# A fused attention and quantised-MLP layer: stationary latents with streamed probabilities, and a rounding add moved to GpSimd

## What is computed

```python
xn   = (x - mean(x)) / sqrt(var(x) + 1e-5)
# attention: 8 heads of 64, keys and values from a latent of rank 64
q    = xn @ Wq.T;  latent = xn @ Wkv_down.T
k, v = latent @ Wk_up.T, latent @ Wv_up.T
attn = softmax(q @ k.T / 8) @ v @ Wo.T
# MLP of width 704 whose four operands are quantised to an fp4 grid in blocks of 16 columns
def fp4(a):                       # scale = max|block| / 6; round to 0, .5, 1, 1.5, 2, 3, 4, 6
    ...
h    = silu(fp4(xn) @ fp4(w_gate).T) * (fp4(xn) @ fp4(w_up).T)
out  = x + attn + fp4(h) @ fp4(w_down).T
```

## Time and profile before

| | |
|---|---|
| median of 3 runs | 1689.79 us (1688.26 to 1696.55) |
| the profiled execution's own time | 1696.03 us |
| its span (first to last instruction) | 1694.0 us |
| mean granted PE clock | 0.974 of full speed |
| busy: PE, DVE, ACT, POOL | 1577.0, 1340.1, 708.9, 517.8 us |

### The profile page before, as it was taken

The page is one execution under the profiler, slowest core; times in us unless marked ns, Lnnn a source line. Parts: engine busy times, 40 slices in busy tenths (PEclk is TensorE's granted clock), DMA queues, the critical chain, the costliest instruction groups (busy, mean ns, idle before and its releaser), DMA issues.

```text
span 1694.0 us, 30412 instructions
## 1 busy us (share of the span) xinstructions
PE 1577.0 (93%) x10726; PEld 1442.1 (85%) x10726; DVE 1340.1 (79%) x3368; ACT 708.9 (42%) x1382; POOL 517.8 (31%) x696
## 2 busy tenths in 40 slices
PE   0599999999999999999999999999999999999998
PEld 0488998989889898988989899898989989898897
DVE  8788787888888888888878788878888877787663
ACT  2444444444444444444443444444344444344432
POOL 7433232332232233323223323223233322332211
PEclk9799999999999999999999999999999999999999
DMA  3000000000000000000000000000000000000000
GB/s 98 7 10 4 8 20 4 19 8 11 14 8 17 7 20 7 10 14 7 17 7 20 4 14 14 8 17 7 20 5 14 14 4 20 7 11 8 1 14 13
DMA packets 22885, 22.60 MB, mean 13 GB/s; under 512 B 3280, under 2 KB 22224, under 8 KB 22736
## 3 DMA queue, kind: packets, MB, share of 16 engines
q1 hardware_dynamic: 22736, 20.65, 4.0%
HBM read 11.99 MB, written 8.39 MB: 12 GB/s over the span
## 4 chain that ended last, share of the span: by engine, by line
PE 87%; DVE 9%; issue 3%; ACT 1%; DMA 0%; POOL 0%; SPq 0%; DVEq 0%; POOLq 0%
PE m L774 35%; PE po L904 23%; PE mx L863 7%; PE st L889 7%; PE st L890 6%; PE m L876 3%; PE m L1010 2%; PE m L1016 1%; PE m L928 1%; DVE row_max L611 1%; PE m L1024 1%; DVE hid L595 1%; DVE on_lo L745 1%; DVE h_small L583 1%; DVE x_small L583 1%
## 5 line engine op out<-in xcount | busy, mean ns | idle before, releaser
L904 PEld LDWEIGHTS po<-lat_tok,probs 128*128 128x128 f32 x4096 | 523.5, 194 | 22.9
L904 PE MATMUL po<-lat_tok,probs 128*128 128x65 f32 x4096 | 519.1, 270 | 0.0
L506 ACT ACTIVATE probs<-st 128x512 f32<-128x512 f32 x512 | 291.3, 595 | 338.2 <-PE st L890 338.2
L611 DVE TENSOR_REDUCE row_max<-mx 128x1 f32<-128x512 f32 x512 | 327.7, 682 | 0.6 <-PE mx L863 0.6
L411 POOL TENSOR_TENSOR h_norm<-hid,h_small 128x352 f32<-128x352 f32 x128 | 100.8, 788 | 480.7 <-DVE h_small L588 480.7
L889 PE MATMUL st<-q_hi,lat 128*128 128x512 f32 x512 | 212.7, 415 | 0.0
L890 PE MATMUL st<-q_lo,lat 65*128 65x512 f32 x512 | 203.6, 398 | 0.0
L774 PE MATMUL m<-wgu_hi,xt_hi 128*128 128x352 f32 x512 | 191.9, 375 | 0.1
L724 DVE TENSOR_TENSOR q_lo<-m,q_hi 64x512 fp32r<-64x512 f32 x128 | 88.1, 688 | 122.4 <-ACT q_hi L546 122.4
L442 POOL TENSOR_TENSOR h_norm<-h_norm,hid 128x352 f32<-128x352 f32 x128 | 119.7, 935 | 211.6 <-DVE h_norm L597 211.6
L863 PE MATMUL mx<-lat,q_hi 128*128 128x512 f32 x512 | 176.5, 426 | 4.0 <-DVE row_max L611 3.9
(11 more groups left out here) (178 smaller groups left out, 3054.2 us busy)
## 6 DMA issues: line engine op xcount, KB each, us to landing
x_in<-in_L_attn_x_dram SPq DMA_DIRECT2D x64, 128.0 KB, 2.2
out_dram<-acc SPq DMA_DIRECT2D x32, 256.0 KB, 2.3
q_lo<-neg_max SPq DMA_DIRECT2D x128, 2.0 KB
weights_in<-in_L_ffn_w_down_dram SPq DMA_DIRECT2D x1, 704.0 KB, 6.3
weights_in<-in_L_ffn_w_gate_dram SPq DMA_DIRECT2D x1, 640.0 KB, 4.7
acc<-in_L_ffn_w_up_dram SPq DMA_DIRECT2D x1, 640.0 KB, 5.9
wq_in<-in_L_attn_Wq_dram SPq DMA_DIRECT2D x1, 512.0 KB, 5.9
x_in<-in_L_attn_Wo_dram SPq DMA_DIRECT2D x1, 512.0 KB, 7.0
```

Of the source, the lines that this page charges most:

```text
L506: act.activation(probs[:, t.c % 2, kc, :], st[kc % 2][:, :], ACT.Exp).then_inc(exp_done, 1)
L611: dve.tensor_reduce(row_max[:, u.c % 2, qc:qc + 1], mx[qc % 2][:, :], AX.X, ALU.max).then_inc(mx_taken, 1)
L904: last = pe.matmul(po[:, qc * P:qc * P + R + 1], probs[:, u.c % 2, kc, qc * P:(qc + 1) * P], lat_tok[:, s.c % 2, kc, 0:R + 1], start=(kc = ...
```

## The change

Five things, in one edit.

1. **Weighing.** `weigh` runs once for two heads, in even slots. `lat_tok` (64 columns) is stationary and `probs` streams: 512 fp32 columns for each block of 128 keys. The first head writes partitions 0 to 63 of `po`, the second 64 to 127, and the two alternate. The result has features on the partitions, as the output product wants it, and the transposes of L1016 go.
2. **Denominators.** POOL adds the four key blocks of `probs` (`add_keys`, three adds of 128x512 for a head); PE multiplies the sum by the ones column, with the sum stationary (64 columns with a stride of 8) and one moving column (`weights_sum`, 16 matmuls for a pair); DVE takes the reciprocal; SP stores it to DRAM and reads it back spread over 64 partitions (`inv_b`); DVE multiplies `po` by it in the next slot; two slots later ACT and POOL split it into `on_hi` and `on_lo`.
3. **Queries.** ACT copies the query product in one piece of 128 partitions (`qp_hi`), DVE makes `qp_lo` in one, and SP places them by six DMAs for a pair. The product itself stands earlier in the slot.
4. **Quantisation.** The rounding constant comes from ACT (a square and a copy with a bias, to bf16), and POOL adds it, where DVE did all three steps. Chunks are normalised two slots earlier.
5. **Order.** The down product is done once for both halves, in odd slots; the residual is loaded into `acc` by a DMA of its own; gate, up and the transposes of maxima and hidden chunk stand together; `wov` moves one slot later. There are 14 lead and 6 tail slots.

```diff
-        on = sb("on", [P, 2, CH, P])
+        on = sb("on", [P, T])
+        inv_b = sb("inv_b", [P, T])
+        key_sum = sb("key_sum", [P, 2, T])
...
+            def place_query(m, u):
+                h = 2 * m.c % QH + u
+                sp.wait_ge(q_hi_done, m.n(1, 1))
+                if u and m.over(2).any():
+                    sp.wait_ge(st_psum, m.n(2 * CH, -2 * CH))
+                for v in range(2):
+                    sp.dma_start(q_hi[v * R:(v + 1) * R, h, :].bitcast(F32), qp_hi[u * R:(u + 1) * R, :].bitcast(F32)).then_inc(q_hi_placed[u], 16)
+                sp.wait_ge(q_lo_done, m.n(1, 1))
+                sp.dma_start(q_lo[0:R, h, :].bitcast(F32), qp_lo[u * R:(u + 1) * R, :].bitcast(F32)).then_inc(q_lo_placed[u], 16)
...
+                m = scaled_pair(t)
+                if m is not None:
+                    sp.wait_ge(inv_done, m.n(1, 1))
+                    sp.dma_start(inv_rows[m.c % 2].rearrange("v (p j) -> (v p) j", p=R), inv_den[:, m.c % 2, :]).then_inc(inv_stored, 16)
...
+                if m is not None:
+                    sp.wait_ge(inv_stored, m.n(16, 16))
+                    for v in range(2):
+                        sp.dma_start(inv_b[v * R:(v + 1) * R, :],
+                                     inv_rows[m.c % 2, v:v + 1, :].broadcast_to([R, T])).then_inc(inv_spread, 16)
...
+            def add_keys(t, kc):
+                total, last = key_sum[:, t.c % 2, :], probs[:, t.c % 2, kc, :]
+                pool.wait_ge(exp_done, t.n(CH, kc + 1))
...
+                pool.tensor_tensor(total, first, last, ALU.add).then_inc(sum_step, 1)
...
-                    pool.wait_ge(h_round, w.n(ROUND_STEPS, ROUND_STEPS))
+                    pool.wait_ge(h_magic_done, w.n(1, 1))
...
-                    pool.tensor_tensor(h_norm[:, :], h_norm[:, :], hid[:, w.c % 2, :], ALU.subtract).then_inc(h_grid, 1)
+                    pool.tensor_tensor(h_norm[:, :], h_norm[:, :], h_magic[:, :], ALU.add).then_inc(h_round, 1)
+                    pool.wait_ge(h_round, w.n(1, 1))
+                    pool.tensor_tensor(h_norm[:, :], h_norm[:, :], h_magic[:, :], ALU.subtract).then_inc(h_grid, 1)
...
+                    act.activation(hid[:, w.c % 2, :], h_norm[:, :], ACT.Square, scale=MAGIC_SQUARE).then_inc(h_square, 1)
+                    act.wait_ge(h_square, w.n(1, 1))
+                    act.activation(h_magic[:, :], hid[:, w.c % 2, :], ACT.Copy, bias=MAGIC_LEAST).then_inc(h_magic_done, 1)
...
+            def weigh(t):
+                m = weighed_pair(t)
+                if m is not None:
...
+                    for kc in range(CH):
+                        pe.wait_ge(exp_done, m.n(2 * CH, CH + kc + 1))
+                        for v in range(2):
+                            last = pe.matmul(po[v * R:(v + 1) * R, :], lat_tok[:, s.c % 2, kc, 0:R], probs[:, v, kc, :],
+                                             start=(kc == 0), stop=(kc == CH - 1))
+                        last.then_inc(pv_done, 1)
...
+                    for j in range(T // R):
+                        for v in range(2):
+                            last = pe.matmul(m2[v * R:(v + 1) * R, j:j + 1],
+                                             key_sum[:, v, :].rearrange("p (q j) -> p q j", j=T // R)[:, :, j],
+                                             lat_tok[:, s.c % 2, 0, R:R + 1], start=True, stop=True)
...
             def slot(t):
                 query_scores(t, 0)
                 query_scores(t, 1)
+                if wov_half(t.plus(-1)) is None:
+                    gate(t)
+                    up(t)
...
+                turn(t)
+                weigh(t)
                 key_scores(t, 0)
                 key_scores(t, 1)
...
                 query_scores(t, 2)
                 query_scores(t, 3)
+                weights_sum(t)
                 key_scores(t, 2)
                 key_scores(t, 3)
...
```

More of the change, by code:

```diff
@@ L208, in transformer_layer @@
         q_lo_done = sem("q_lo_done")
+        q_hi_placed = [sem(f"q_hi_placed{b}") for b in range(2)]
+        q_lo_placed = [sem(f"q_lo_placed{b}") for b in range(2)]
         mx_psum = sem("mx_psum")
@@ L236, in transformer_layer @@
         down_taken = sem("down_taken")
+        res_loaded = [sem(f"res_loaded{c}") for c in range(CH)]
         wov_psum = sem("wov_psum")
@@ L262, in ltok_seq, with weighed_pair, scaled_pair, split_pair @@
             return s if t.c % H == 6 and s.within(B) else None
-        def turned_pair(t):
+        def weighed_pair(t):
             m = t.plus(-2).over(2)
             return m if t.c % 2 == 0 and m.within(B * PAIRS) else None
+        def scaled_pair(t):
+            m = t.plus(-3).over(2)
+            return m if t.c % 2 and m.within(B * PAIRS) else None
+        def split_pair(t):
+            return weighed_pair(t.plus(-2))
+        def down_chunk(t):
+            n = t.plus(-5).over(2)
+            return n if t.c % 2 and n.within(B * CH) else None
         def wov_half(t):
             s = t.over(H).plus(-1)
[L272 to L276, removed]
+            m = s.times(2, t.c % H - 2)
+            return m if t.c % H in (2, 3) and m.within(B * 2) else None
+        LEAD = [At(c) for c in range(-14, 0)]
+        TAIL = [At(SLOTS + c) for c in range(6)]
         def lead_slots(slot):
@@ L890, in key_scores @@
                     pe.matmul(st[kc % 2][:, :], lat1[:, s.c % 2, keys], q_lo[:, h, :], start=False, stop=True).then_inc(st_psum, 1)
-            def weigh(t, n):
-                u, kc = (t.plus(-1), n + 2) if n < 2 else (t, n - 2)
-                if u.within(SLOTS):
-                    s = u.over(H)
-                    if kc == 0:
-                        if u.any():
-                            pe.wait_ge(on_done, u.n())
-                        pe.wait_ge(ltok_done, s.n(1, 1))
-                    pe.wait_ge(exp_done, u.n(CH, kc + 1))
-                    for qc in range(CH):
-                        last = pe.matmul(po[:, qc * P:qc * P + R + 1], probs[:, u.c % 2, kc, qc * P:(qc + 1) * P],
-                                         lat_tok[:, s.c % 2, kc, 0:R + 1], start=(kc == 0 and qc == 0),
-                                         stop=(kc == CH - 1), skip_group_check=True)
-                    last.then_inc(pv_done, 1)
@@ new lines, in weights_sum @@
+            def weights_sum(t):
+                m = weighed_pair(t)
+                if m is not None:
+                    s = m.over(PAIRS)
+                    if t.plus(-2).within(SLOTS) or t.plus(1).within(SLOTS):
+                        turned_taken(t)
+                    else:
+                        m2_free(t.plus(-1))
+                    pe.wait_ge(sum_step, m.n(2 * (CH - 1), 2 * (CH - 1)))
+                    for j in range(T // R):
[3 more added lines that the diff above has]
+                                             lat_tok[:, s.c % 2, 0, R:R + 1], start=True, stop=True)
+                    last.then_inc(den_psum, 1)
```

415 lines of the change are left out of this document (226 added, 189 removed).

## The result

The changed kernel takes 1678.88 us (median of 8 runs, 1674.07 to 1685.93), the one before 1691.01 (8 runs, 1687.97 to 1696.55): a ratio of 0.993, 95% interval 0.991 to 0.995. That is 0.7% faster where 4.7% was forecast. The profiled execution has a span of 1679.7 us (before 1694.0) and a mean granted clock of 0.935 (before 0.974).

The account below looks back on a forecast made before the run. PE was taken as the bound: 22.6 us of work, 0.75 query wait and 0.1 other waits made 23.4 a pair. 64 x 23.4 plus 119 lead and tail led to 1610 us, own range 1510 to 1690, whole range 1500 to 1790.

Parts of the forecast that it names:

- PE as the bound, and its old period: PE's work per slot sets the time; the old period is 24.7 us for a pair of slots.
- PE's fixed work: PE's unchanged work: 6.4 us a slot, and 16.5 a pair with the terms done once per pair or sequence.
- Streamed weighing: PE's 16 weighing instructions of 512 columns overlap by halves: 3.9 us a pair, plus 0.3 for filling and draining.
- the ninth step: In the streamed weighing, one step of 0.43 us for the offset, added to eight overlapped steps.
- Denominators, as PE work: PE's 32 one-column denominator instructions at 0.06 us each: 1.9 us a pair, with ends 1.7 and 3.4.
- I drop the 1.0 of waits and low clock, but for 0.1.: Of the old period's 1.0 us a pair of PE waits and low clock, only 0.1 would remain.
- Queries by DMA: PE waits for transferred queries before the next slot's query scores: 0.75 us a pair, ends 0 and 2.5.
- Lead and tail: Time outside the steady periods: 113 us as before, and 6 more for query hops and the longer end chain.
- POOL: POOL's work grows to 20.7 us a pair and fits; rival, POOL needs 24.4 and bounds, median 1676, 10%.
- The halves in turn.: Rival: in even slots' weighing the two halves do not overlap, 3.0 us more a pair, median 1772; 28%.
- The DMA hops as the bound.: Rival: SP issues the queries late, PE waits 2.5 us instead of 0.75 and the clock falls, median 1751; 7%.

Follow-up runs that it names:

- e12: e8 with SP issuing the spread of the reciprocal ahead of placing the maxima, as in e11; 1545.85 us, ratio 0.913 to the kernel before.
- e8: Changed kernel with the 64-column denominators of e1 and the gate-first order of e6 together; 1562.35 us, ratio 0.924 to the kernel before.
- e3: Changed kernel, but weighing does all four key blocks of the first head, then the second's, instead of alternating; 1784.61 us, ratio 1.055 to the kernel before.
- e1: Changed kernel with the denominator instructions streaming 64 columns instead of 1, same count; 1617.99 us, ratio 0.956 to the kernel before.
- e6: Changed kernel with PE doing the gate product before the first two query scores, where the bank allows it; 1614.72 us, ratio 0.956 to the kernel before.
- e11: Changed kernel with SP issuing the spread of the reciprocal ahead of placing the maxima; 1632.76 us, ratio 0.965 to the kernel before.
- e4: Changed kernel with DVE instead of POOL adding the rounding constant for h and x; 1680.92 us, ratio 0.993 to the kernel before.
- e10: e8 with DVE instead of POOL adding the rounding constant for h and x; 1560.03 us, ratio 0.923 to the kernel before.
- e2: Changed kernel with 28 of a pair's 32 denominator instructions left out, so its output is wrong; 1508.91 us, ratio 0.891 to the kernel before.
- e5: Changed kernel with the 32 one-column denominator instructions in two stretches of 16, key scores between; 1687.92 us, ratio 0.998 to the kernel before.

## Why the prediction was wrong, point by point

The forecast was 1610 us (its own range 1510 to 1690), the result 1678.88: the direction held, the size did not. That 1678.88 lies in the range is luck: its high end stood for denominators of 3.4 us a pair, and they took 2.02.

**PE as the bound, and its old period.** Right: 24.7 us a pair, and down to e12 everything that shortened PE's path shortened the kernel.

**PE's fixed work.** The terms of a slot that the prediction lists add up to 6.28 us, not 6.4, so the 16.5 that stay are 0.24 a pair too much. The error hid among smaller ones: e8, where PE hardly waits, has a period of 22.4 a pair against the 22.6 of the sum.

**Streamed weighing.** The mechanism was right, and two of its sizes were wrong in opposite ways. The two halves start 0.007 us apart, so the ninth step that I added for an offset is not there: eight steps of 0.429 are 3.43, not 3.9. What the two half-width stretches cost at their ends was taken as 0.3 and is about 0.6. The medians over all 64 pairs show it: the first weighing instruction starts 0.203 us behind the transpose where transposes stand 0.109 apart, its first step is 0.48 and its last 0.52 instead of 0.43, and the first key score behind it takes 0.34 instead of 0.23. That is 0.3 at each of the two stretches; the denominators show nearly the same distances. The sum of the three terms, 3.9 + 0.3 + 1.9, comes out by luck. The Trainium skill, TensorEngine Tiling (Array Packing), Tiling Modes, says that different tiles work in parallel and that a change of mode drains the array. By e3 and by the starts, the trace agrees with the first; with the second it agrees in sign, though no run shows that the 0.3 is a drain.

**Denominators, as PE work.** Right: 2.02 against 1.9 us, 0.06 for an instruction.

**The step that failed: "I drop the 1.0 of waits and low clock, but for 0.1."** I counted the low clock of before as a consequence of the wait at L1024 that goes, and gave the new stretch of 32 one-column matmuls only its length. It also lets the clock fall: 171 us at the lower level in the steady state, at most 85 us of lost time; e1 measures 61 us for it, 0.95 a pair. The forecast's own sign for being right, a clock of 0.97 or more, failed with 0.935. The old part of the term did go: away from the new stretches 5 falls are left where there were 9. With the clock held up, e1's 1618 us is within 0.5% of the 1610 forecast, so this is nearly the whole miss. That they are so close is in part luck: e1's period is 23.17 us a pair against 23.45 in the sum, 18 us less over 64 pairs, and its lead and tail take 130 us against 119. No row of the kernel before has a one-column stretch in it. What the earlier trace rows could have told me is that a full busy share does not mean a full clock (970 to 974 us, at 0.50). I had seen that the clock falls behind a stretch in which PE waits, and did not ask what it does behind one in which PE is "busy" with one column at a time.

**Queries by DMA.** The size was near, the place was wrong. A wait at the first query scores of even slots was there; with the clock held up it cost 56 us (e1 to e8), 0.87 a pair against the 0.75 of the sum. But PE waited longer for row maxima, held up by the spread reciprocal. The prediction has the two hops end "halfway through the odd slot, where DVE needs them". In the chain shown with e6 they end at 885.07, 8.9 us into an odd slot of 11.3 (876.18 to 887.45). SP's order made them late, which e11 shows with 46 us.

**Lead and tail.** 21 us more, not 6. The first latent is rounded at 74.8 instead of 65.8 us, which is 9 of them, and the other 12 come at the end. No run separates the causes.

**POOL.** Right: 1214.2 busy, 1220 said; key sums 1.28 us each, 1.27 said. It is no bound in the changed kernel nor in e8, and the add that moved to it is worth nothing (e4, e10). The rival's price is wrong as well: it said that POOL needs 24.4 us a pair, and in e2 it keeps up with 21.6. There, though, it leads the chain (54%), so it stands close behind PE.

**The halves in turn.** Not the case here. In e3, made to order, the overlap shrinks and the kernel is slower than before, as the rival's sign had it; its 6.9 us was too pessimistic, since half of the overlap stays (12 steps between 8 and 16).

**The DMA hops as the bound.** In part what happened, by another transfer and at a lower price.

## What to carry to other kernels

The stretch of one-column matmuls cost twice: once for its length, and again because work behind it ran at half clock, while PE's busy share showed neither. Widening the moving side to 64 columns, most of which are never read, cost 0.07 us a pair and kept the clock up. Whether that holds where the loads are not what limits such instructions, no run shows. Look at the granted clock next to each stretch, not at the busy share. And in an in-order queue that only issues DMAs, put the transfer with the longest chain behind it first: moving one issue ahead of one wait gave 46 us here, while taking 147 us of work from an engine that bounds nothing gave none.

## What the runs showed of the hardware that I had not expected

- PE took an instruction for the other half of the array ahead of three that stand before it in its program (e3: doubled starts from 817.53 us on, and the same in all 63 complete stretches). How far ahead it can look was not tried.
- Each half-width stretch costs about 0.3 us more than its steps (starts of the changed kernel), and a third such stretch in a pair of slots another 0.28 (e5).
- Two such denominator instructions, one for each half, come every 0.12 us, with 1 moving column and with 64. Their stationary operand has 64 columns with a stride of 32 bytes, and its load is recorded with 216 ns on average, where the packed 64 columns of the weighing have 136. That the loads set the 0.12 us is likely but not shown.
- DVE's reciprocal took 3358 ns for 512 columns, about 6.5 ns a column; a multiplication of the same shape 691 ns.
